# Attention pass of a graph kernel: bias moved into the indicator product, sigmoid read from PSUM, running sum placed before the next layer's dots

## The chip, the cores and the metric

The kernel runs on one core of a Trainium2 chip. The time is the device time of one execution in microseconds (us); what is compared is the median of several executions. The engines are PE (TensorE), DVE (VectorE), ACT (ScalarE), POOL (GpSimd) and SP (SyncE, which here only issues DMAs). Each engine works through its own instructions in order and waits for the others by semaphores.

## The reference, cut to what matters

The program is two graph networks, one after the other, over 100,000 nodes of 128 channels and 50,000 edges sorted by destination. The change touches only the first of them, three layers of graph attention:

```
def _gat_conv(x, src, dst, W, a_src, a_dst, b, n_nodes):
    h = x @ W
    s = h @ a_src
    d = h @ a_dst
    e = s[src] + d[dst]
    e = where(e > 0, e, 0.2 * e)
    w = exp(e - segment_max(e, dst)[dst])
    denom = segment_sum(w, dst)
    alpha = w / (denom[dst] + EPS)
    return segment_sum(alpha[:, None] * h[src], dst) + b
...
for m in range(3):
    x = x + sigmoid(_gat_conv(x, src, dst, Ws[m], att_src[m], att_dst[m], bias[m], n))
```

Every node has a loop to itself beside its edges, so a node without an edge has the closed form x + sigmoid(x @ W + b). The kernel computes that for all nodes in a first stage and then replaces the rows of the nodes that have edges.

## The kernel before

**Stages.** A dense stage over all nodes takes the first 1400 us. Then each of the three layers m has two passes over the edges: a first pass that gathers the source rows and takes their dots with the attention vectors, a short chain that turns scores into weights (`w`, denominators `slU`, their reciprocals), and a second pass that sums the rows and writes the new ones. After 6400 us comes the second network, which the change leaves alone. The change touches the second passes.

**Rounds.** The edges are cut into 392 columns of 128, and U = 8 columns make a round, so each pass has R = 49 rounds. `p_rounds` writes the first three rounds out, then a hardware loop whose body is four rounds, then the last ones. Inside `p2_round(i, rr, h)` every engine handles pieces of up to four different rounds, so the program is a software pipeline: for layer m, r = m * R + i.

**PE**, in the order of a round i: the product of the running sums of round i-1 with W into `pCW`'s PSUM bank (L1188, needs the scan of round i-1); the sums of round i, eight pairs of products `bXs x pA` and `pXd x bSW` (L1194, L1195, need masks and diagonals of round i); for round i-1 eight pairs `pAT x W` and `pIN x pCW` (L1204, L1206); the keys of round i+2 laid out along the columns (L1180). `pIN` holds in rows 0 to 7 an indicator of which column still belongs to the segment that a running sum carries on; all other rows are zero.

**ACT**: copies `pCW` (L955), copies the sums of round i out of PSUM to `pAT` (L964), writes eight diagonal matrices `bSW` for round i+1 (L949), and takes the sigmoid of round i-1 in place in SBUF, two groups of four columns (L970). In the last layer it first applies eight ReLUs with the normalisation of round i-2 (L959).

**DVE**: copies key fields for round i+2 (L1629); masks `pA` of round i+1 (L1637); for round i-2, in layers 0 and 1, sixteen dots with the next layer's attention vectors (L1653, L1655) and their copy to `SC` (L1659); copies `pFL` (L1663); the running sum of round i (`scan`, L1461, needs ACT's copy of the sums of round i); for round i-1 eight times PSUM * 1/denominator + bias into `bTH` (L1675, semaphore p_z); then, once the scatter of two rounds earlier has left the buffer, the addition of the node's own row (L1689). In the last layer come the second residual and the normalisation statistics (L1694 to L1706).

**POOL** issues eight indirect scatters for each round, one for each column (L770); in the last layer it first computes the reciprocal deviations (L783 to L787). **SP** issues in a round i: two loads of rows for round i+1 (L520, L523), the indicator of round i (L538), and in layers 0 and 1 the store of the new rows of round i-1 (L548). In the last layer it loads the residual rows too (L544).

## Time and profile before

| what | us |
|---|---|
| median of 3 runs | 13333.38 (13315.89 to 13337.69) |
| the profiled execution | 13224.56 |
| its span, first to last instruction | 13222.7 |
| second pass of layer 0, about | 2649 to 3410 |
| second pass of layer 1, about | 4060 to 4800 |
| second pass of layer 2, about | 5440 to 6410 |

The profiled execution is 0.8% below the median of the runs. Shares of the span: PE 51%, DVE 39%, ACT 30%, POOL 50%. They are averages over stages with different limits, so that the second passes are read by themselves: by windows inside them, by the waits in those windows, and by single rounds of the timeline. A wait "<-issue" or "<-remote" is idle time that the profile puts down to nothing, or to no engine of this core.

### The profile page before, as it was taken

Reading aid. Unit: us, or ns where it says so; the run is one execution under the profiler, and the core shown is the slowest. Engines: PE = TensorE matmul, PEld = TensorE weight load, DVE = VectorE, ACT = ScalarE, POOL = GpSimd, SP = SyncE. Lnnn points to the kernel's source line nnn. Section 1 sums busy time; section 2 is a strip of 40 time slices with the busy share of each in tenths; the row PEclk is TensorE's granted clock in tenths of the full one; section 3 lists DMA queues with packets and bytes.
Section 4 is the critical chain, followed back from the end, with each engine's and each line's share of the span. In section 5 each row is a group of like instructions: output and inputs, shape, how many; then the busy total and the mean of one; then the engine's idle time right before and its main releaser. Section 6 shows DMA issues by size and latency. Waiting matters only on the chain.

```text
span 13222.7 us, 165920 instructions
## 1 busy us (share of the span) xinstructions
PE 6805.4 (51%) x35028; PEld 5020.9 (38%) x35028; DVE 5117.0 (39%) x21443; ACT 3990.4 (30%) x8589; POOL 6568.4 (50%) x6253
## 2 busy tenths in 40 slices
PE   6777200077205730355322247777445888444888
PEld 3333100066205630355322235555333555333666
DVE  6777422366315641455322234443112333111444
ACT  7999300033102310233200024443112444111443
POOL 3444566544664566444677743233665333665000
PEclk9999655588657865677555568888556999555999
DMA  6777666644574457533233345565445777444998
GB/s 219 264 262 264 220 237 237 227 126 125 194 261 158 129 174 257 179 119 121 67 45 45 45 117 201 202 202 189 60 58 128 240 234 236 83 58 88 272 268 256
DMA packets 2128228, 2270.53 MB, mean 172 GB/s; under 512 B 234960, under 2 KB 1554869, under 8 KB 2121824
## 3 DMA queue, kind: packets, MB, share of 16 engines
q1 hardware_dynamic: 1798266, 1848.65, 42.2%
q0 software_dynamic: 321440, 418.37, 15.0%
q10 hardware_dynamic: 8390, 2.21, 0.1%
q14 instruction: 105, 0.86, 0.0%
q8 instruction: 27, 0.44, 0.0%
HBM read 1067.73 MB, written 1222.73 MB: 173 GB/s over the span
## 4 chain that ended last, share of the span: by engine, by line
DMA 14%; issue 11%; PE 8%; another core or an unknown queue 5%; POOL 4%; DVE 4%; SPq 3%; POOLq 1%; DVEq 0%; ACT 0%; ACTq 0%
DMA agg_d<-dO,fOI 10%; PE ps L1290 5%; DMA bXd<-agg_d 3%; POOL bO L810 2%; POOL agg_d L801 2%; PE ps L1267 2%; SPq L595 1%; DVE aO L1809 1%; PE ps L1277 1%; DVE bXd L1782 1%; PE ps L1265 1%; SPq L593 1%; DVE eE L1803 1%; SPq L602 0%
## 5 line engine op out<-in xcount | busy, mean ns | idle before, releaser
L862 POOL DMA_INDIRECT bXs<-x_d,fGI x784 | 798.6, 1019 | 1494.8 <-DMA x_d<-aH 1279.9
L801 POOL DMA_INDIRECT agg_d<-dO,fOI x784 | 1212.1, 1546 | 530.9 <-ACT dO L982 296.9
L1290 PE MATMUL ps<-W,aT 128*128 128x128 f32 x9408 | 1206.4, 291 | 22.8 <-ACT aS L999 15.6
L1277 PE MATMUL ps<-aS,W1X 128*128 128x512 f32 x2352 | 1207.4, 594 | 5.4 <-DMA eET<-eaT_d 5.2
L1290 PEld LDWEIGHTS ps<-W,aT 128*128 128x128 f32 x9408 | 1181.7, 208 | 39.7 <-ACT aS L999 25.9
L982 ACT COPY dO<-ps 128x128 f32<-128x128 f32 (+1 forms) x1176 | 318.2, 271 | 2733.7 <-DMA agg_d<-dO,fOI 1526.6
L1817 DVE TENSOR_TENSOR aH<-ps,B 128x512 f32<-128x512 f32 x588 | 406.4, 692 | 1848.1 <-PE ps L1290 1151.8
L1246 PE MATMUL ps<-bO,bNE 128*128 128x128 f32 x1568 | 568.9, 473 | 1021.5 <-ACT dO L982 1010.0
L1005 ACT ACTIVATE aT<-ps,BNT,BNS 128x512 f32<-128x512 f32 x1176 | 882.4, 774 | 609.2 <-PE ps L1278 574.7
L747 POOL DMA_INDIRECT bXs<-x_d,bGI x784 | 784.3, 1000 | 392.8 <-issue 247.7
L1246 PEld LDWEIGHTS ps<-bO,bNE 128*128 128x128 f32 x1568 | 382.5, 305 | 1198.1 <-issue 912.2
L1511 DVE CUSTOM_DVE_ANT_0 bTL<-bXs,VR 128x128 f32<-128x128 f32 x1176 | 290.1, 288 | 1411.6 <-DMA bXs<-x_d,bGI 803.2
L942 ACT ACTIVATE aYG<-aYG 98x512 f32<-98x512 f32 x3 | 1.9, 630 | 2444.1 <-DVEq L1605 2444.1
L1064 PE MATMUL ps<-aT,W 128*128 128x512 f32 x1176 | 616.1, 619 | 181.4 <-DVE aT L1411 181.3
L1733 DVE TENSOR_SCALAR bNE<-ps,dK 128x128 f32<-128x128 f32 x1176 | 317.7, 343 | 1007.8 <-PE ps L1224 1005.4
L801 POOL DMA_INDIRECT agg_d<-dO,dOI x392 | 618.7, 1578 | 153.4 <-issue 118.2
L770 POOL DMA_INDIRECT x_d<-bO,bOI x400 | 395.5, 989 | 519.3 <-DVE bO L1689 398.5
L1267 PE MATMUL ps<-ident,aO 128*128 128x128 f32 x2352 | 425.2, 321 | 365.8 <-DVE aO L1809 340.4
L1094 PE MATMUL ps<-ident,SC 128*98 128x128 f32 x12 | 3.3, 428 | 1173.4 <-DVEq L1570 1173.4
L1195 PE MATMUL ps<-bSW,bXd 128*128 128x128 f32 x2352 | 593.3, 343 | 26.4 <-issue 26.4
L1094 PE MATMUL ps<-ident,self_score 128*98 128x128 f32 x12 | 3.3, 430 | 1170.7 <-DVEq L1556 1170.7
L1012 ACT ACTIVATE aH<-aH 128x512 f32<-128x512 f32 x392 | 246.7, 630 | 1082.7 <-DVE aH L1817 713.5
(260 smaller groups left out, 17793.7 us busy)
## 6 DMA issues: line engine op xcount, KB each, us to landing
agg_d<-zeros SPq DMA_DIRECT2D x788, 256.0 KB
bXd<-agg_d SPq DMA_DIRECT2D x784, 256.0 KB
agg_d<-zeros SPq DMA_DIRECT2D x394, 290.0 KB
bXd<-agg_d SPq DMA_DIRECT2D x392, 290.0 KB
x_d<-aO SPq DMA_DIRECT2D x392, 256.0 KB, 2.1
yg_d<-aYG SPq DMA_DIRECT2D x196, 512.0 KB, 3.1
aX<-yg_d SPq DMA_DIRECT2D x392, 256.0 KB, 4.2
x_d<-aH SPq DMA_DIRECT2D x392, 256.0 KB
```

The lines of the kernel that those rows point to most:

```text
L747: pool.indirect_dma_start(bXs[:, s, u, :], None, gat_src[m], bass.IndirectOffsetOnAxis(ap=bGI[:, s, 1 if m == 0 else 0, u:u + 1], axis=0), ...
L770: pool.indirect_dma_start(gat_out[m], bass.IndirectOffsetOnAxis(ap=bOI[:, s, u:u + 1], axis=0), bOs[s][:, u, 0:wid], None, bounds_check=n_ ...
L801: pool.indirect_dma_start(agg_d[m][u % 2], bass.IndirectOffsetOnAxis(ap=index, axis=0), dO[:, u, 0:AW[m]], None, bounds_check=agg_last, oo ...
L862: pool.indirect_dma_start(fX[:, s, u, 0:C], None, gin_in[m], bass.IndirectOffsetOnAxis(ap=fGI[:, s, u:u + 1], axis=0), bounds_check=n_last ...
L1005: act.activation(eZ[:, k, h, :], ps[2 + 2 * k + h][:, :], ACT.Relu, bias=BNT[:, m, h:h + 1], scale=BNS[:, m, h:h + 1]).then_inc(e_zr, 1)
L1064: pe.matmul(ps[2 + k][:, :], W[:, m, :], aT[:, k, m, :], start=True, stop=True).then_inc(a_mm, 1)
L1195: mm = pe.matmul(cols(2 + u // 4, u % 4), pXd[:, rr, u, :], bSW[:, u, :], start=False, stop=True)
L1246: pe.matmul(ps[2 + u % 4][:, 0:C], dS[:, u, :], message_slot(s)[:, u, :], start=True, stop=True).then_inc(d_acc, 1)
L1267: mm = pe.transpose(ps[k][:, j * P:(j + 1) * P], eS[:, k, j, :], ident[:, :])
L1277: pe.matmul(z, W1X[:, m, h * P:(h + 1) * P], eHT[:, k, :], start=True, stop=False)
L1290: mm = pe.matmul(ps[6 + k][:, j * P:(j + 1) * P], eZ[:, k, h, j * P:(j + 1) * P], W2[:, m, h, :], start=(h == 0), stop=(h == 1))
L1817: v.tensor_tensor(eO[:, k, :, :], ps[6 + k][:, :].rearrange("p (j c) -> p j c", j=J), bias, ALU.add).then_inc(e_v, 1)
```

## The change

The bias is no longer added by DVE. The denominators, already in the slab `slU`, are stored to a DRAM buffer `den_d`; each round loads its eight columns of them as one row into partition 32 of `pIN`, and partition 32 of `pCW` holds the layer's bias. The product L1206, which always ran over 128 rows, then adds denominator * bias, and the later multiplication by the reciprocal leaves the bias. ACT takes the sigmoid straight from PSUM with the reciprocal as scale column, eight instructions of 128 columns, and does so before the diagonals of the next round. DVE loses L1675; its copy of `pFL` and its scan stand before the dots. SP issues one more DMA in each round, and at the start of each pass stores `den_d`, waits for it, and issues the first row loads only once the denominators stand.

```diff
+    den_d = dram("den_d", (R, U * P))
...
 SP, round i
                         sp.dma_start(pIN[0:U, s, :], ind_d[bass.ds(i, 1), :, :].rearrange("o u n -> (o u) n")
                                      ).then_inc(l_ix[s], 16)
+                        sp.dma_start(pIN[32:33, s, :], den_d[bass.ds(i, 1), :]).then_inc(l_ix[s], 16)
...
 SP, start of a pass
+                sp.wait_ge(z_v, ZV * (m + 1))
+                sp.dma_start(den_d.rearrange("r (h n) -> (r h) n", h=2), slU).then_inc(s_den, 16)
                 load_rows_of(0, 0)
+                sp.wait_ge(s_den, 16 * (m + 1))
...
 ACT, round i
+                    if inside(i - 1):
+                        act.wait_ge(p_fl, r)
+                        if past(i - 2):
+                            act.wait_ge(p_o, 2 * (r - 1))
+                        for u in range(U):
+                            if u % 4 == 0:
+                                act.wait_ge(p_rw, 2 * (r - 1) + u // 4 + 1)
+                            ins = act.activation(bTH[:, u, :], ps[4 + u // 4][:, (u % 4) * P:(u % 4 + 1) * P], ACT.Sigmoid,
+                                                 scale=pFL[:, 1 - s, 1, u:u + 1])
+                            if u % 4 == 3:
+                                ins.then_inc(p_sg, 1)
                     if inside(i + 1):
                         diagonals(i + 1, 1 - s)
-                    if inside(i - 1):
-                        for g in range(2):
-                            act.wait_ge(p_z, 2 * (r - 1) + g + 1)
-                            act.activation(bTH[:, 4 * g:4 * g + 4, :], bTH[:, 4 * g:4 * g + 4, :], ACT.Sigmoid).then_inc(p_sg, 1)
...
 ACT, start of a pass
+                act.copy(pCW[32:33, :], GB[32:33, m, :]).then_inc(p_cb, 1)
...
 PE, round i
                         if past(i - 2):
-                            pe.wait_ge(p_z, 2 * (r - 1))
+                            pe.wait_ge(p_sg, 2 * (r - 1))
...
 DVE, round i: the block "if inside(i)" (pFL, scan) now stands before the block of the dots; and
-                    if inside(i - 1):
-                        for u in range(U):
-                            if u % 4 == 0:
-                                v.wait_ge(p_rw, 2 * (r - 1) + u // 4 + 1)
-                            ins = v.scalar_tensor_tensor(out=bTH[:, u, :], in0=ps[4 + u // 4][:, (u % 4) * P:(u % 4 + 1) * P],
-                                                         scalar=pFL[:, 1 - s, 1, u:u + 1], in1=GB[:, m, :], op0=ALU.mult,
-                                                         op1=ALU.add)
-                            if u % 4 == 3:
-                                ins.then_inc(p_z, 1)
```

ACT, one round in the loop of layer 0, before. `pCW` and `bA` are the copies out of PSUM, `bSW` the diagonals of the next round, `bTH` the argument of the sigmoid.

```order
L955 COPY pCW<-ps 8x128 [waits p_cw]
L963 ISA
L964 COPY bA<-ps 128x512 [waits p_ag]
L963 REGISTER_ALU
L964 COPY bA<-ps 128x512 [waits p_ag]
L947 REGISTER_ALU
L949 ACTIVATE bSW<-ident,pFE 128x128 [waits p_fe]
L949 ACTIVATE bSW<-ident,pFE 128x128 x7
L970 ACTIVATE bTH<-bTH 128x512 [waits p_z] x2
```

The same round of ACT in the changed kernel.

```order
L961 COPY pCW<-ps 8x128 [waits p_cw]
L969 ISA
L970 COPY bA<-ps 128x512 [waits p_ag]
L969 REGISTER_ALU
L970 COPY bA<-ps 128x512 [waits p_ag]
L978 ACTIVATE bTH<-ps,pFL 128x128 [waits p_rw,p_o,p_fl]
L978 ACTIVATE bTH<-ps,pFL 128x128 x3
L978 ACTIVATE bTH<-ps,pFL 128x128 [waits p_rw]
L978 ACTIVATE bTH<-ps,pFL 128x128 x3
L953 REGISTER_ALU
L955 ACTIVATE bSW<-ident,pFE 128x128 [waits p_fe]
L955 ACTIVATE bSW<-ident,pFE 128x128 x7
```

The sigmoids moved ahead of the diagonals, became eight, and wait for PE's products (p_rw) in place of DVE's (p_z).

DVE, from the end of the dots to the end of a round in the loop of layer 0, before.

```order
L1659 ISA [waits p_dt]
L1659 COPY SC<-bDT 128x2x8
L1663 ISA [waits p_z]
L1663 COPY pFL<-keys 128x16
L1668 COPY pC<-pC 128x1 [waits p_c,p_fl,p_ev]
L1461 SCALAR_TENSOR_TENSOR pC<-pFL,pC,bA 128x8
L1674 REGISTER_ALU
L1675 SCALAR_TENSOR_TENSOR bTH<-ps,pFL,GB 128x128 [waits p_rw]
L1675 SCALAR_TENSOR_TENSOR bTH<-ps,pFL,GB 128x128 x3
L1674 REGISTER_ALU
L1675 SCALAR_TENSOR_TENSOR bTH<-ps,pFL,GB 128x128 [waits p_rw]
L1675 SCALAR_TENSOR_TENSOR bTH<-ps,pFL,GB 128x128 x3
```

The changed kernel, from the end of the masks to the first dots.

```order
L1654 TENSOR_SCALAR aH<-ps,pFE 128x128 x3
L1667 REGISTER_ALU
L1668 ISA [waits p_sg]
L1668 COPY pFL<-keys 128x16
L1673 COPY pC<-pC 128x1 [waits p_c,p_fl,p_ev]
L1478 SCALAR_TENSOR_TENSOR pC<-pFL,pC,bA 128x8
L1681 ISA bTL,bDT<-bO,VR 128x128 [waits p_dc,p_o]
```

The scan (L1461, now L1478) stands between masks and dots, and nothing follows the dots but their copy and the last addition.

## Rows read from the trace of the kernel before

**Rows 1.** Windows in the three passes: length, busy PE, PEld, DVE, ACT, POOL (xcount), clock, DMA share, GB/s

```profile
2700.00:3340.00 640.00, 460.83 (x2991) 408.96 (x2990) 414.92 (x2267) 199.33 (x529) 316.16 (x322) 0.81 0.43 128
4110.00:4750.00 640.00, 480.29 (x3120) 424.26 (x3119) 432.75 (x2352) 206.19 (x546) 331.39 (x337) 0.83 0.42 132
5500.00:6300.00 800.00, 466.07 (x2893) 425.43 (x2894) 405.92 (x1618) 300.97 (x826) 393.74 (x434) 0.73 0.35 121
```

**Rows 2.** Groups by line, 2700 to 3340: xcount | busy us, mean ns | idle before

```profile
L770 POOL DMA_INDIRECT x_d<-bO,bOI x162 | 159.8, 986 | 180.7 <-DVE bO L1689 131.5 <-issue 49.2
...
L949 ACT ACTIVATE bSW<-ident,pFE 128x128 f32<-128x128 f32 x328 | 100.2, 391 | 0.0
L1675 DVE SCALAR_TENSOR_TENSOR bTH<-ps,pFL,GB 128x128 f32<-128x128 f32 x320 | 86.6, 343 | 27.6 <-remote 24.7 <-PE ps L1206 3.0
...
L970 ACT ACTIVATE bTH<-bTH 128x512 f32<-128x512 f32 x80 | 50.4, 630 | 255.5 <-DVE bTH L1675 252.6 <-issue 3.0
...
L1659 DVE COPY SC<-bDT 128x16 f32 x40 | 7.0, 175 | 88.6 <-remote 83.6 <-issue 2.9 <-DVE bDT L1655 2.1
```

**Rows 3.** Groups by line, DVE, 4110 to 4750

```profile
L1663 DVE COPY pFL<-keys 128x16 f32 x42 | 8.2, 195 | 0.0
```

**Rows 4.** Waits, 2700 to 3340: who waited for whom, us in total, times, longest

```profile
POOL x_d L770 <- DVE bO L1689: 131.5, 20, 11.0
PE ps L1180 <- issue: 121.1, 135, 4.3
...
DVE SC L1659 <- remote: 83.6, 27, 4.3
DVE pFE L1629 <- issue: 68.9, 10, 7.5
...
PE ps L1188 <- DVE pC L1461: 32.9, 13, 6.0
```

**Rows 5.** Waits, 4110 to 4750

```profile
DVE SC L1659 <- remote: 92.4, 33, 3.6
...
PE ps L1188 <- DVE pC L1461: 21.8, 8, 6.4
```

**Rows 6.** Timeline of a round of layer 0: start, length, engine, line [idle before]

```profile
2935.53 2.45 ACT L949 ACTIVATE bSW<-ident,pFE 128x128 f32<-128x128 f32 x8
...
2948.11 0.23 DVE L1461 TENSOR_TENSOR_SCAN pC<-pFL,pC,aYG 128x8 f32<-128x8 f32 x1
...
2948.92 0.80 PE L1194 MATMUL ps<-bNE,bXs 128*128 128x128 f32 x2
...
2950.39 1.40 DVE L1689 TENSOR_TENSOR bO<-bTH,bXd 128x512 f32<-128x512 f32 x2
```

**Rows 7.** Timeline, the end of that round

```profile
2959.19 0.27 PE L1180 MATMUL ps<-ident,pFE 128*128 128x128 f32 x1 [0.46 <-issue]
...
2962.85 0.17 DVE L1659 COPY SC<-bDT 128x16 f32 x1 [2.89 <-remote]
```

**Rows 8.** Timeline of a round of layer 2

```profile
5850.62 3.18 ACT L959 ACTIVATE aT<-aT,bNR,bRS 128x128 f32<-128x128 f32 x8 [12.49 <-POOL bNR L787]
...
5851.31 1.09 POOL L770 DMA_INDIRECT yg_d<-bO,bOI  x1 [0.73 <-ACT aT L959]
...
5863.02 0.17 DVE L1686 COPY bOI<-IDX 128x8 int32 x1 [5.88 <-DMA yg_d<-bO,bOI]
...
5868.63 0.24 POOL L783 TENSOR_SCALAR bRS<-bMV 128x8 f32<-128x8 f32 x1 [7.27 <-DVE bNG L1706]
```

**Rows 9.** Timeline, from the denominators of layer 0 to its first rounds

```profile
2636.93 3.35 DVE L1620 RECIPROCAL aYG<-aYG 98x512 f32<-98x512 f32 x1
...
2648.81 0.63 PE L1194 MATMUL ps<-bNE,bXs 128*128 128x128 f32 x2
...
2653.93 1.04 PE L1180 MATMUL ps<-ident,pFE 128*128 128x128 f32 x8
```

**Rows 10.** The page, 40 slices of the span: GB/s that the DMA engines moved

```profile
GB/s 219 264 262 264 220 237 237 227 126 125 194 261 158 129 174 257 179 119 121 67 45 45 45 117 201 202 202 189 60 58 128 240 234 236 83 58 88 272 268 256
```

More of the change, by code:

```diff
@@ L1216, in _ @@
                 keys_along(1, 1)
+                pe.wait_ge(p_cb, m + 1)
                 p_rounds(pe, p2_round)
@@ L1647, in p2_round @@
                         masks(i + 1, 1 - s)
+                    if inside(i):
+                        if past(i - 2):
+                            v.wait_ge(p_sg, 2 * (r - 1))
+                        v.tensor_copy(pFL[:, s, :, :], keys[:, 4:6, bass.ds(i * U, U)]).then_inc(p_fl, 1)
+                        v.wait_ge(p_ev, 2 * (r + 1))
+                        v.wait_ge(p_fl, r + 1)
+                        if m or past(i - 1):
+                            v.wait_ge(p_c, r)
+                        v.tensor_copy(pC[:, s, 0:1], pC[:, 1 - s, U:U + 1])
+                        scan(pC[:, s, 1:U + 1], pFL[:, s, 0, :], pAT[s][:, P - 1:U * P:P], pC[:, 1 - s, U:U + 1], ALU.mult,
+                             ALU.add).then_inc(p_c, 1)
                     if inside(i - 2) and m < M - 1:
@@ L1659, in p2_round @@
                         v.tensor_copy(SC[:, 1:3, bass.ds((i - 2) * U, U)], bDT[:, 0:2, :]).then_inc(p_dc, 1)
-                    if inside(i):
-                        if past(i - 2):
-                            v.wait_ge(p_z, 2 * (r - 1))
-                        v.tensor_copy(pFL[:, s, :, :], keys[:, 4:6, bass.ds(i * U, U)]).then_inc(p_fl, 1)
-                        v.wait_ge(p_ev, 2 * (r + 1))
-                        v.wait_ge(p_fl, r + 1)
-                        if m or past(i - 1):
-                            v.wait_ge(p_c, r)
-                        v.tensor_copy(pC[:, s, 0:1], pC[:, 1 - s, U:U + 1])
-                        scan(pC[:, s, 1:U + 1], pFL[:, s, 0, :], pAT[s][:, P - 1:U * P:P], pC[:, 1 - s, U:U + 1], ALU.mult,
-                             ALU.add).then_inc(p_c, 1)
-                    if inside(i - 1):
-                        for u in range(U):
-                            if u % 4 == 0:
-                                v.wait_ge(p_rw, 2 * (r - 1) + u // 4 + 1)
-                            ins = v.scalar_tensor_tensor(out=bTH[:, u, :], in0=ps[4 + u // 4][:, (u % 4) * P:(u % 4 + 1) * P],
-                                                         scalar=pFL[:, 1 - s, 1, u:u + 1], in1=GB[:, m, :], op0=ALU.mult,
-                                                         op1=ALU.add)
-                            if u % 4 == 3:
-                                ins.then_inc(p_z, 1)
                     if inside(i - 1):
@@ L1711, in _ @@
                 p_rounds(v, p2_round)
+                v.wait_ge(s_den, 16 * (m + 1))
                 if m < M - 1:
```

9 lines of the change are left out of this document (6 added, 3 removed).

## The prediction

> **What bounds the kernel now.** The change touches only the second passes of the three layers, so I read windows inside them first, then the groups and waits of the same windows, then single rounds of the timeline.
>
> In layer 0 the window of 640 us holds 40 rounds, since the copy at L1659 runs once in a round: 16.0 us a round. Layer 1 does 42 rounds in 640 us: 15.2 us [rows 1 to 3]. In layer 2 POOL does 11 instructions in a round (three for the deviations, eight scatters), 434 in 800 us: 39.5 rounds of 20.3 us [rows 1]. No engine is full. Per round of layer 0, PE is busy 460.83 / 40 = 11.5 us, DVE 10.4, ACT 5.0 [rows 1]. POOL's scatter takes 0.99 us and 49.2 / 162 = 0.30 us of issue, so eight need 10.3 us [rows 2]. That is the floor of a round however fast the rest is; POOL now also waits for DVE's last addition, 131.5 us in 20 of the 40 rounds, those of one buffer [rows 4].
>
> The remainder of a round is of two kinds. One is waiting for DVE. PE waits for the scan 32.9 us in 40 rounds, 0.82 us a round, in layer 1 21.8 / 42 = 0.52 us [rows 4, 5]. ACT waits for the bias step 252.6 us [rows 2], but that is ACT's rest, not the path. The other kind I call the slow stretch: near the end of a round several engines crawl together. The keys, eight short products, need 1.04 us when nothing hinders them [rows 9], yet they sit idle 121.1 / 40 = 3.0 us a round with no releaser, each product standing 0.4 us and more after the one ahead [rows 4, 7]. In the same microseconds DVE stands 2.89 us ahead of the copy after the dots, 83.6 / 40 = 2.1 us a round, and 92.4 / 42 = 2.2 in layer 1 [rows 4, 5, 7]. PE's 11.5 busy + 3.0 crawling + 0.8 waiting is 15.3 of the 16.0 us, and DVE's 10.4 + 2.1 + 1.7 at the loop's turn + 0.7 ahead of the bias step is 14.9. So both chains are nearly closed, and PE's is the longer one. This is what I build on: a microsecond taken from DVE is worth only what PE waits for DVE.
>
> Layer 2 is another loop. POOL has the deviations; ACT's ReLUs follow at 5850.62, the scatters of the round before start at 5851.31, eight times 1.28 us; DVE, idle 5.88 us, is let into the buffer at 5863.02 when they have landed; its additions and statistics end at 5868.63 with the next deviations [rows 8]. None of these steps is L1675.
>
> **The change, part by part.**
>
> *Bias step gone from DVE, scan ahead of the dots.* It removes eight instructions, 86.6 / 40 = 2.2 us of DVE a round [rows 2], and lets the scan run as soon as ACT has copied the sums, ahead of sixteen dots. PE's wait for the scan should vanish: 49 x 0.82 + 49 x 0.52 = 66 us over layers 0 and 1. DVE's chain falls to 12.7 us, so what is late next is PE itself. The bound on the other side: the crawl stays where it is and PE, arriving earlier, only crawls longer; then a half or none of it is won. I take the whole, because the longest waits for the scan (6.0 us, 6.4 us) are too long to be hidden in a 3 us crawl. -66 us, ends -66 and 0.
>
> *Eight sigmoids for two on ACT.* No row shows a sigmoid of 128 columns from PSUM. The nearest below is the diagonal, 128 columns with a scale column, eight in 2.45 us [rows 6]; above, the ReLU with scale and bias columns, eight in 3.18 us [rows 8]. Now they are 2 x 0.63 = 1.3 us [rows 2]. I take 2.45, since the operands are those of the diagonal but for the source: ACT goes from 5.0 to 6.2 us of busy time, far from full.
>
> *Sigmoids ahead of the diagonals.* This is a new wait, and what is queued behind it on ACT is the eight diagonals that PE needs for the next sums. The sigmoids wait for PE's last products of the round. After those come four sigmoids and the first diagonal, 4 x 0.31 + 0.39 = 1.6 us (2.0 with the ReLU's price). PE in that time does the keys, 1.04 us, and the step from scan to first sum, 2948.34 to 2948.92, 0.6 us: also 1.6 us [rows 6, 9]. So the new wait is 0 to 0.4 us a round; with the hop of a semaphore I take 0.2: 98 x 0.2 = +20 us, ends 0 and +39. If PE's keys crawl, they cover it whole; if the products themselves come late, see the slow rival.
>
> *The bias row.* One more DMA of 4 KB a round on SP. It is issued behind the indicator of the same round and needed a round later, as that is; queued behind it on SP are the store and the loads of the next but one round. The product L1206 ran over 128 rows before, so PE pays nothing. 0; were SP on the path, an issue of about half a microsecond would be 98 x 0.5 = +49 us, which belongs to the slow rival.
>
> *Start of a pass.* The first row loads now wait for the denominators. From the end of the reciprocals, 2640.28, to the first sum, 2648.81, are 8.5 us [rows 9]. Two loads of 512 KB at the window's 128 GB/s would need 8.2 us, at the 264 GB/s of the dense slices 4.0 us [rows 10]. I take 1 us for three passes, upper end 3 x 2: +1, ends 0 and +6.
>
> *Layer 2.* ACT's diagonals move 2.4 us later, and so do PE's sums; DVE's idle 5.88 us ahead of the buffer and PE's rest until the next masks (PE is busy 466.07 / 39.5 = 11.8 of 20.3 us [rows 1]) hide it. 0.
>
> Sum: -66 + 20 + 1 = -45 us. Against the profiled execution that is 13224.56 - 45 = 13180 us. The median of the runs lies 109 us above that execution; I assume that this offset is not in the second passes and put the same -45 on the median: **13288 us**. The forecast's own range is 13267 (-66) to 13345 (half the gain, all costs: -33 + 39 + 6).
>
> **The rivals.**
>
> *The crawl sets the round (no change).* If all engines advance at a common pace, the number of instructions decides. The windows hold 9099 and 9474 of them [rows 1], 227 and 226 a round. The change takes away eight and adds six: 1% of 15.6 us, 0.14 us, times 98 is -14: 13320. For it: all engines crawl at once, and the crawl is in both layers alike. Against it: equal counts, yet 0.8 us between the layers' rounds. 20%.
>
> *The loop's turn.* DVE stands 68.9 us in layer 0, ten times for up to 7.5 us, once every four rounds, ahead of L1629 with nothing to wait for [rows 4]; in layer 1 it does not, and that layer's round is 0.8 us shorter. The loop bodies of DVE shrink in the changed program, from 263 instructions to 231 in layer 0 and from 273 to 241 in layer 1. If the stand goes with that, layer 0 falls to layer 1's pace: 49 x 0.8 = 37 us, of which 49 x 0.3 = 15 are already in the scan waits. -45 - 22: 13266. 12%. The Trainium skill, in "Runtime: NRT & Kernel Launch", section "Instruction fetch mechanics", states that instructions come in blocks of 256, that most engines hold two, and that a branch to a block no longer held waits for a fetch. By that rule 231 instructions always fit in two blocks, 263 not always, and the stand goes; the trace shows that it is there in one layer and not in the other, not why.
>
> *DVE was the bound (much faster).* If the crawl is made by DVE and PE running densely together, thinning DVE shortens it, and a round may fall to 13 us, half way to POOL's 10.3. 49 x (3.0 + 2.2) = -255: 13078. For it: the crawl comes where keys and dots meet. Against it: PE's part, 14.5 us, has no DVE in it. 12%.
>
> *ACT becomes the bound (slower).* So far ACT writes the diagonals right after its copies of the sums, while PE still has its last products to do. Changed, they sit behind those products; where the crawl falls on those, all eight sigmoids, 2.4 to 3.2 us, and the first diagonal stand between the end of the crawl and the next sum, where PE has 1.6 us of its own: 1.2 to 2.0 us lost. In two of three rounds that is 98 x 0.67 x 1.6 = +105, the scan's gain being lost too since PE then waits for diagonals instead; with a little given back, +90: 13423. It decides the sign once PE waits over 66 / 98 = 0.7 us a round for diagonals. 17%.
>
> **How the numbers follow.** The forecast has 39%, the rivals 20, 12, 12 and 17. The predicted time is the forecast's. The range must leave out no more than 2 in 10: 13130 cuts off the "much faster" case (10%), 13400 most of the slow one (9%). About 0.2%, 27 us, is what a measurement of this kernel can tell from no change. Faster by more than that: 0.29 of the forecast's 0.39 and both faster rivals, 0.53. Within it: 0.20 and 0.09 from the forecast and its edge, 0.29. Slower: 0.17 and a little, 0.18.
>
> **What would show it.** Right: PE no longer waits for the scan in layers 0 and 1, the round is 15 us in both, layer 2 stays at 20.3, the crawl is still there with 2 to 3 us a round on PE. Wrong: PE waiting for ACT's diagonals by more than 0.7 us (slow rival), a crawl much shorter (fast rival), a wait for `bXs` or `pXd` in the first round of a pass, or a layer 2 round that moved. If no loop of DVE stands at its turn any more, that rival was right too.

## The result, and the profile after

The changed kernel takes 13364.17 us (median of 9 executions, 13353.29 to 13371.48), the kernel before in the same comparison 13327.59 us (median of 9): a ratio of 1.0023 with a 95% interval of 1.0015 to 1.0032. It is slower by 37 us, where 45 us of gain were forecast. The two were later compared twice more, on chips called C and E below: 1.0007 (0.9998 to 1.0015) and 1.0012 (1.0003 to 1.0022). So the change costs nothing to 0.3%, and the question is where the gain went.

The profiled execution took 13364.17 us, with a span of 13362.6. The windows of the three second passes, to be held against [rows 1] (columns: length, busy PE, PEld, DVE, ACT, POOL, each with its count, then clock, DMA share, GB/s):

```profile
2720.00:3360.00 640.00, 446.21 (x2935) 407.10 (x2936) 332.30 (x1897) 231.48 (x760) 310.92 (x315) 0.79 0.42 124
4150.00:4790.00 640.00, 441.32 (x2988) 403.13 (x2986) 340.06 (x1958) 233.95 (x769) 319.15 (x323) 0.81 0.41 129
5580.00:6380.00 800.00, 473.56 (x2896) 431.65 (x2896) 322.71 (x1291) 341.31 (x1069) 394.44 (x433) 0.71 0.34 120
```

DVE got what it was promised: 332.30 / 40 rounds = 8.3 us instead of 10.4. ACT rose from 5.0 to 5.8 us. PE is less busy than before in 640 us, so it waits more. Layer 2 did not move: 433 instructions of POOL in 800 us, 20.3 us a round.

What PE and ACT waited for from 2700 to 3340 (who, for whom, us in total, times, longest), beside [rows 4]:

```profile
PE ps L1210 <- ACT bSW L955: 121.7, 24, 8.2
...
PE ps L1196 <- issue: 14.9, 20, 1.7
PE ps L1204 <- issue: 6.2, 9, 1.2
```

```profile
ACT bTH L978 <- remote: 157.7, 25, 10.0
```

The wait for the scan is gone: the product with the running sums, L1204, is never behind DVE. The slow stretch left the keys too, L1196, 14.9 us instead of 121.1. In their place stands one line: PE waits for ACT's diagonals (L955) ahead of the sums (L1210), 121.7 us, 3.0 us a round; layer 1 has the same line with 125.6 us in 30 waits. And ACT stands 157.7 us ahead of its sigmoids (L978), in 25 pieces of up to 10 us, with nothing that the profile can name.

Two groups by line, 2720 to 3360 (xcount, busy us, mean ns, idle before):

```profile
L978 ACT ACTIVATE bTH<-ps,pFL 128x128 f32<-128x128 f32 x320 | 89.4, 379 | 174.5 <-remote 157.7 <-PE ps L1222 8.6 <-issue 8.1
...
L1646 DVE COPY pFE<-keys 128x24 f32 x40 | 7.0, 174 | 35.0 <-ACT bSW L955 34.8 <-issue 0.2
```

The sigmoids themselves are cheap, 89.4 / 40 = 2.2 us a round for eight. The loop of DVE no longer stands at its turn: 0.2 us of issue ahead of L1646, where 68.9 stood ahead of L1629 [rows 4].

A round of layer 0 from the timeline (start, length, engine, line, in brackets the idle time ahead):

```profile
2958.58 0.39 PE L1222 MATMUL ps<-pCW,aO 128*128 128x128 f32 x2
...
2958.80 1.04 PE L1196 MATMUL ps<-ident,pFE 128*128 128x128 f32 x8
...
2961.33 0.29 DVE L1681 CUSTOM_DVE_ANT_0 bTL<-aT,VR 128x128 f32<-128x128 f32 x1 [0.61 <-issue]
...
2962.04 0.29 DVE L1683 CUSTOM_DVE_ANT_0 dO<-aT,VR 128x128 f32<-128x128 f32 x1 [0.41 <-issue]
...
2964.93 2.18 ACT L978 ACTIVATE bTH<-ps,pFL 128x128 f32<-128x128 f32 x8 [8.91 <-remote]
...
2966.94 2.47 ACT L955 ACTIVATE bSW<-ident,pFE 128x128 f32<-128x128 f32 x8
2967.51 0.50 PEld L1210 LDWEIGHTS ps<-bNE,bXs 128*128 128x128 f32 x2 [7.52 <-issue]
2967.54 0.77 PE L1210 MATMUL ps<-bNE,bXs 128*128 128x128 f32 x2 [7.35 <-ACT bSW L955]
```

By its record PE's last product of the round ends at 2958.97, and the keys, at full speed now, take 1.04 us. ACT might start its sigmoids then, but the slow stretch comes (DVE gets out one instruction in 0.71 us, the two dot products above), and ACT's first sigmoid starts at 2964.93. Then come eight sigmoids, 2.2 us, and only behind them the first diagonal, at 2966.94. PE has stood for 7.35 us.

What ACT stood for can be read, though no view prints it: the packed trace also keeps the time at which each semaphore was raised. The product that frees the first four sigmoids ends by its record at 2957.18, but its semaphore is raised at 2964.90, and the first sigmoid starts 0.03 us later; for the second four it is 2958.96 and 2965.80. Of the products of the round before, the last ends at 2948.77 and its semaphore is raised at 2948.78, so the two can also stand together. So ACT waits for PE's products, and their signal is up to 7.7 us late. Whether the products themselves were late or only their signal is not shown, since the ends of products are modelled.

About every second round goes like this one (24 waits for the diagonals in 40 rounds). In the others the stretch falls on PE's products and on ACT's copy of the sums. From one round's sums to the next it is about 15 and 17 us, mostly in turns. What comes in turns of 8.4 and 23 us in this trace are the running sums (L1478, at 2948.48, 2956.86 and 2980.35), which are not rounds; the expectation of `after_3` further down takes them for rounds.

### The profile page after: what moved, and what is told of

It reads as the page before. It is cut to its first block, busy times and chain, and to the rows that moved or that the text cites. A ratio compares the mean times of both kernels' runs of the same rounds, so it can differ in the third digit from the quotient of the medians.

```text
span 13362.6 us, 166188 instructions
## 1 busy us (share of the span) xinstructions
PE 6799.2 (51%) x35028; PEld 5047.7 (38%) x35028; DVE 4823.4 (36%) x20267; ACT 4127.8 (31%) x9474; POOL 6584.4 (49%) x6253
## 3 DMA queue, kind: packets, MB, share of 16 engines
q0 software_dynamic: 321440, 418.37, 14.9%
## 4 chain that ended last, share of the span: by engine, by line
DMA 14%; issue 11%; PE 8%; another core or an unknown queue 5%; DVE 4%; POOL 4%; SPq 3%; POOLq 1%; DVEq 0%; ACT 0%; ACTq 0%
DMA agg_d<-dO,fOI 10%; PE ps L1307 5%; DMA bXd<-agg_d 4%; POOL bO L816 2%; POOL agg_d L807 2%; PE ps L1284 2%; SPq L601 1%; DVE bXd L1791 1%; DVE aO L1818 1%; PE ps L1294 1%; SPq L599 1%; PE ps L1282 1%; DVE eE L1812 1%; SPq L608 0%
```

## How the experiments are read

The comparisons fell on different chips, here A to E; A is that of the first one, and whether it is one of the others is not known. The kernel before takes 13328 us on A, 13263 on B, 13266 and 13263 on C, 13261 on E and 12320 on D, so that only ratios to it on the same chip are compared. The table gives the length of a second pass in the profile of each kernel, from its first to its last product of the diagonals (L1195 of the kernel before), and in brackets that length / 48, the round. Each length is that of one execution; the same kernel differs in it by up to 12 us between chips for both layers together (1457 to 1469 us before).

| kernel | chip | layer 0, us | layer 1, us | ratio to before, 95% interval |
|---|---|---|---|---|
| before | A | 750.8 (15.64) | 718.5 (14.97) | |
| changed | A | 765.5 (15.95) | 755.4 (15.74) | 1.0023 (1.0015 to 1.0032) |
| base_again: before | B | 745.5 (15.53) | 711.8 (14.83) | 0.9994 (0.9985 to 1.0003) |
| early_sum_only | B | 752.4 (15.68) | 707.0 (14.73) | 0.9984 (0.9975 to 0.9993) |
| late_sum | B | 710.8 (14.81) | 707.7 (14.74) | 0.9951 (0.9938 to 0.9965) |
| dg_first | B | 688.9 (14.35) | 687.1 (14.31) | 0.9918 (0.9904 to 0.9932) |
| after_again: changed | C | 739.7 (15.41) | 743.7 (15.49) | 1.0007 (0.9998 to 1.0015) |
| late_dg | C | 712.0 (14.83) | 710.5 (14.80) | 0.9963 (0.9950 to 0.9976) |
| one_dot | C | 694.7 (14.47) | 680.5 (14.18) | 0.9935 (0.9919 to 0.9950) |
| half_rows | C | 691.9 (14.41) | 679.4 (14.15) | 0.9933 (0.9916 to 0.9951) |
| four_sc | C | 513.5 (10.70) | 504.0 (10.50) | 0.9653 (0.9635 to 0.9670) |
| one_scatter | C | 455.6 (9.49) | 438.9 (9.14) | 0.9536 (0.9521 to 0.9551) |
| before_one_sc | C | 563.9 (11.75) | 500.0 (10.42) | 0.9674 (0.9657 to 0.9691) |
| after_one_sc | C | 456.0 (9.50) | 445.1 (9.27) | 0.9549 (0.9532 to 0.9566) |
| quarter_rows | D | 475.7 (9.91) | 469.5 (9.78) | 0.9887 (0.9871 to 0.9902) |
| paused | D | 513.4 (10.70) | 505.5 (10.53) | 0.9966 (0.9953 to 0.9978) |
| base_3: before | E | 748.4 (15.59) | 718.2 (14.96) | 1.0002 (0.9993 to 1.0012) |
| after_3: changed | E | 738.6 (15.39) | 744.2 (15.50) | 1.0012 (1.0003 to 1.0022) |
| dg_first_3 | E | 685.4 (14.28) | 679.0 (14.15) | 0.9926 (0.9910 to 0.9943) |
| paused_3 | E | 688.2 (14.34) | 667.9 (13.91) | 0.9923 (0.9907 to 0.9940) |

Layer 2's pass lies between 944 and 948 us in every one of them. The profiled execution of `early_sum_only` was the slowest of its eleven (13270 us, median 13240), so its lengths do not show what its ratio shows. `after_again` was expected at 1.0015 to 1.0032 with rounds of 15.7 to 16.0 us; it came out at 1.0007 with 15.4 and 15.5.

## The order on ACT and on DVE

Theory A: the late diagonals are the new bottleneck. Theory B: all engines share a pace set by the number of instructions, and no order matters. The first four runs should separate them.

> The kernel before, unchanged, for a profile of one of its ordinary executions (the one shown of before, 13224.6 us, lay 0.8% under its other times). All theories: 13316 to 13340 us. New wait (A): the second passes of layers 0 and 1 take 751 and 719 us here as in the first profile, so that the change added 15 and 37 us to them. Own pace (B: the stretches in which all engines slow down set the mean round, whatever the order): they take some 10 to 25 us longer than in the first profile, because that one was a lucky execution, and the change then added less than 40 us in both together.

It is the kernel before, unedited. Its passes are 5 and 7 us shorter than in the first profile, not longer; about half of that is the chip (13263 against 13328 us). So the first profile was no lucky one in the second passes. What made that execution fast was not looked for.

`dg_first`, on ACT in `p2_round`:

```
+                    if inside(i + 1):
+                        diagonals(i + 1, 1 - s)
                     if inside(i - 1):
                         act.wait_ge(p_fl, r)
...
                                 ins.then_inc(p_sg, 1)
-                    if inside(i + 1):
-                        diagonals(i + 1, 1 - s)
```

> The changed kernel, with ScalarE's eight diagonals put ahead of the eight sigmoids again; nothing else. New wait (A: TensorE stands 3.0 us a round for diagonals because the sigmoids, which now wait for TensorE's own product, stand ahead of them): that wait goes, the round of layers 0 and 1 falls from 15.8 to at most 15.0 us, and the kernel takes 13280 us or less (36.5 to 80 us under 13364). Own pace (B): the wait for diagonals goes as well, but the slow stretch falls on another wait (keys again, or the masks), the round stays at 15.5 to 15.9 us and the kernel at 13350 to 13375 us.

13149.74 against 13262.87 us. Two lines moved, and the round falls from between 15.4 and 15.9 us to 14.3. Theory B expected no change and falls. The ratios, 0.9918 against 1.0007 to 1.0023 for the changed kernel, put the gain at 0.9 to 1.1%, more than A's own 0.3 to 0.6%.

`late_sum`: the block with the copy to `pFL` and the scan goes behind the dots again, where it was before.

> The changed kernel, with the running sum behind the dot products again; bias row and sigmoid from PSUM stay. Order as forecast (my prediction): TensorE waits again 0.8 us a round for the scan, +66 us less what the other waits hide: 13400 to 13430 us. Own pace (B): no difference, 13350 to 13375 us. New wait (A): between, since TensorE now stands for the diagonals behind the sigmoids and these wait for the product that the scan releases: 13364 to 13400 us.

13198.02 us, 0.9951. All three expectations missed: undoing the early sum makes the changed kernel faster. So the early sum is harmful beside late diagonals. What PE waited for from 2700 to 3340:

```profile
PE ps L1222 <- issue: 68.9, 101, 1.2
PE ps L1220 <- issue: 66.1, 97, 1.2
PE ps L1210 <- ACT bSW L955: 8.2, 13, 1.8
```

With the sum late, the slow stretch falls on PE's products themselves, 135 us in small pieces. By the time they are done it is over, and ACT's sigmoids and diagonals follow at once: 8.2 us of wait instead of 121.7. With the sum early, the records of PE's products have ended when the stretch comes, their signal is late, and the sigmoids ahead of the diagonals wait for it.

`early_sum_only`: the same block of the kernel before, moved ahead of its dots; bias step and sigmoids as before.

> The kernel before, with only the running sum moved ahead of the dot products. Order as forecast: TensorE's wait for the scan (0.8 and 0.5 us a round) goes, 13328 - 66 = 13262 us. New wait (A): the sigmoids stay behind the diagonals here, so nothing takes the gain away: 13262 to 13300 us. Own pace (B): 13315 to 13340 us, as before, with the slow stretch somewhere else.

13240.47 us, 0.9984: 22 us of gain, under A's 28 to 66, and more than B's none. Neither was right. PE, from 2700 to 3340:

```profile
PE ps L1194 <- issue: 68.8, 21, 4.8
PE ps L1194 <- DMA bXd<-xhc_d: 44.5, 13, 4.3
```

The scan is no longer waited for here either, but the stretch and the row loads now stand ahead of the sums, for 2.8 us a round.

`late_dg`: both moves undone, bias row and sigmoid from PSUM kept.

> The changed kernel with both orders as they were before: diagonals ahead of the sigmoids, running sum behind the dots; bias row and sigmoid from PSUM stay. It completes a square: after 15.9 us a round (sum early, diagonals late), diagonals first 14.35, sum late 14.8. Each order has its own price (A): the wait of TensorE for the scan comes back on top of the version with the diagonals first, 14.35 + 0.8 = 15.1 us a round, ratio 0.996 to 0.998. Only the pair early sum and late diagonals is bad (C: the sum ahead of the dots lets the product run early, sigmoids and diagonals then meet the slow stretch): this one is within 0.2 us a round of the version with the diagonals first, ratio 0.991 to 0.993.

0.9963, in the range of A in this text (each order has its own price, 0.996 to 0.998); its round of 14.8 us is under A's 15.1 and more than 0.2 us over 14.35, C's limit. PE's wait for the scan, 32.9 us in this window before, is 13.3 us here. So the four corners are, with the sum late, 14.8 us a round whichever way ACT is ordered, and with the sum early 14.3 us with diagonals first and 15.4 to 15.9 us with diagonals last. The two moves of the change are one gain and one loss that only exists with the gain.

## What the slow stretch is

`one_dot` is `dg_first` with only one of the 16 dot products of a round left, so that the next layer's weights come from stale numbers:

```
-                        for u in range(U):
-                            v.tensor_tensor_reduce(bTL[:, u, :], bOs[s][:, u, 0:C], next_d, ...
+                        for u in range(U - 1, U):
```

> Diagonals first, and of the 16 dot products of each round of layers 0 and 1 only one is left (15 VectorE instructions and 3 us of its time less a round; the softmax of the next layer gets stale numbers). Slow stretch made by how many instructions all engines issue (B): 288 instructions a round at 20.1 per us become 273, the round falls by 0.75 us, 72 us in 96 rounds, ratio 0.986. VectorE's own chain counts (C): its turn of masks, sum, dots and adds becomes 3 us shorter, up to 2 us a round fall out, ratio 0.977 or less. Neither: ratio as with the diagonals first, 0.992.

0.9935, like `dg_first` (0.9918, 0.9926). The window from 2700 to 3340:

```profile
2700.00:3340.00 640.00, 485.95 (x3243) 432.97 (x3241) 221.80 (x788) 251.79 (x827) 349.18 (x351) 0.84 0.46 139
```

DVE's busy time is 5.0 us a round (221.80 in 351 / 8 = 44 rounds), where the changed kernel has 8.3, and nothing came of it. So with eight scatters and the diagonals first, neither these instructions nor DVE's time sets the round.

A look into the kernel before, on chip E, where the stretch starts (of POOL the fifth, seventh and eighth scatter are shown):

```profile
2956.46 0.98 POOL L770 DMA_INDIRECT x_d<-bO,bOI  x1 [0.30 <-issue]
...
2957.82 0.29 DVE L1655 CUSTOM_DVE_ANT_0 dO<-bO,VR 128x128 f32<-128x128 f32 x1 [0.41 <-issue]
2957.84 0.27 PE L1180 MATMUL ps<-ident,pFE 128*128 128x128 f32 x1 [0.34 <-issue]
2958.53 0.08 DVE L1655 DVE_READ_ACCUMULATOR2_ANT bDT<- 128x1 f32 x1 [0.41 <-issue]
...
2959.03 0.98 POOL L770 DMA_INDIRECT x_d<-bO,bOI  x1 [0.30 <-issue]
2959.26 0.27 PE L1180 MATMUL ps<-ident,pFE 128*128 128x128 f32 x1 [1.15 <-issue]
...
2960.32 0.98 POOL L770 DMA_INDIRECT x_d<-bO,bOI  x1 [0.30 <-issue]
...
2961.41 0.27 PE L1180 MATMUL ps<-ident,pFE 128*128 128x128 f32 x1 [1.13 <-issue]
2962.12 0.37 PE L1180 MATMUL ps<-ident,pFE 128*128 128x128 f32 x1 [0.44 <-issue]
```

The starts are spaced by multiples of 0.71 us on PE and on DVE alike (2957.82 to 2958.53, 2961.41 to 2962.12), whatever the instruction costs. POOL's scatters keep their 1.29 us. ACT is different: from 2957.62 its eight diagonals run in 2.45 us, at full speed, and in 640 us of this trace no two of ACT's instructions follow each other by 0.71 us, against some 66 pairs on DVE. ACT only stands and waits. The slow pace begins at about the fifth of eight scatters and is over about 2 us behind the start of the last. The DMA engines are not full in it: in the changed kernel their share is 0.37 from 2960 to 2967. So the next kernels take scatters away; whoever reads the rows later gets stale ones.

```
                         elif u % 4 == 0:
                             pool.wait_ge(p_o, 2 * (m * R + i) + u // 4 + 1)
+                        if m < M - 1 and u < U - 1:
+                            continue
```

> Diagonals first, and of the 8 scatters of each round of layers 0 and 1 only one is left (7 GpSimd instructions less a round and 7/8 of the scattered rows; the next layer then works on rows that were never written). Slow stretch made by instruction count alone (B): 7 of 288 instructions less, round 14.35 to 14.0 us, ratio 0.989. Slow stretch made by the descriptors or by the DMA traffic of the scatters (D): it goes or shrinks to under half, the round falls to 9 to 12 us, where the dense rounds of 8.4 us are, ratio 0.96 or less.

0.9536: 5 us of every round are gone. Not all of them are the stretch: eight scatters at 1.29 us keep a round at 10.3 us or more, one does not. The same edit in the kernel before and in the changed one:

> The kernel before, with one of the 8 scatters of each round of layers 0 and 1 left (the next layer works on rows that were not written). In its trace all engines fall to one or two instructions a microsecond from about the fifth scatter of a round to two microseconds behind the eighth. Scatters make the slow stretch (D): it goes, and VectorE's own work sets the round, since its eight bias operations are still there (its busy time without the slow stretch is about 9.8 us a round): 10 to 11 us, ratio 0.963 to 0.970. If the slow stretch has another source here: 13 us or more.

> The changed kernel, with one of the 8 scatters of each round of layers 0 and 1 left, as in the kernel before beside it. Without the slow stretch the terms of the prediction stand alone. If its terms (scan wait gone, VectorE 2 us a round freer, a small wait for diagonals) were right and only the slow stretch overturned them: a round of 8.5 to 9.5 us, 1 to 2 us under that of the kernel before with one scatter, ratio 0.950 to 0.956. If the late diagonals cost by themselves: TensorE waits over 0.5 us a round for them here too, and the round is at least 0.5 us over the 9.3 us of the version with the diagonals first.

0.9674 and 0.9549, both in the ranges given, as is the changed kernel's round; the kernel before has 11.75 us in layer 0, where 10 to 11 were expected. Windows from 2700 to 3050, first of `before_one_sc`, then of `after_one_sc`:

```profile
2700.00:3050.00 350.00, 275.89 (x2173) 258.92 (x2172) 296.48 (x1641) 144.35 (x382) 28.75 (x30) 0.91 0.48 140
```

```profile
2700.00:3050.00 350.00, 317.00 (x2739) 301.07 (x2738) 300.68 (x1775) 218.60 (x703) 36.27 (x37) 1.00 0.60 175
```

POOL's count is the number of rounds. In 350 us the kernel before does 30, the changed one 37: 11.7 against 9.5 us. Without the stretch DVE is the limit before: 296.48 of 350 us busy, and 44.1 us of standing at the turn of its loop, in two rows, the second put down to ACT though the stand is as long:

```profile
DVE pFE L1631 <- issue: 25.4, 4, 6.9
DVE pFE L1631 <- ACT bSW L951: 18.7, 3, 6.9
```

The change takes the stand and the eight bias steps away; as a whole it is worth 1.3% here. PE is busy for 317.00 of the 350 us then, and its granted clock is 1.00, the level of 2.4 GHz, where the windows of the kernel before and of the changed one have 0.79 to 0.83 in layers 0 and 1, a mix of both levels. PE's work of a round takes 317.00 / 37 = 8.6 us here and 446.21 / 40 = 11.2 us in the changed kernel with all scatters: 2.6 us a round. In the timeline above, PE stands for 7.35 us and starts again with a granted clock of 0.50, 1.2 GHz, with two products every 0.43 us, and two every 0.22 us from 2972.77 on. The clock does not explain what the late diagonals cost: `dg_first_3` has

```profile
2700.00:3340.00 640.00, 493.79 (x3308) 442.57 (x3308) 374.59 (x2120) 256.50 (x843) 352.74 (x354) 0.85 0.47 140
```

and 45 rounds in it, 11.0 us of PE's work a round, as good as the same. With one scatter, `one_scatter` has 321.04 us in 37 rounds, 8.7: close to half of the 5 us that the scatters cost is PE's own work at the lower clock. In `after_one_sc` PE's wait for the late diagonals is there too, and it is small:

```profile
PE ps L1212 <- ACT bSW L957: 30.5, 34, 1.7
```

That is 0.8 us a round, four times my 0.2, yet the round is within 0.15 us of the 9.49 and 9.14 us of `one_scatter`, which has the diagonals first. The late diagonals become expensive only with the stretch.

The late signals go with the scatters too. From the end of the record of PE's product to its semaphore, the median over layer 0 (2700 to 3340, or to 3050 with fewer scatters and on D) is 4.7 us in the changed kernel on A and 3.0 on E, 5.5 and 5.8 in the kernel before on A and E, 5.7 in `dg_first_3` and 5.6 in `half_rows`; in `late_sum`, where the products themselves crawl, half of the signals are on time. It is 0.01 us in all three versions with one scatter. In layer 2, which has eight scatters a round, it is 0.01 us in every kernel. So eight scatters alone do not make the stretch. Nor does the rate of the others: layer 2 has 10.7 recorded instructions per us, the changed kernel's layer 0 has 13.8, and `after_one_sc` 22.8 without any stretch. What must come together with the scatters was not tested.

> Diagonals first, with 4 of the 8 scatters of each round of layers 0 and 1 left. With 8 the round takes 14.35 us, with 1 it takes 9.3. Each scatter has its price: 9.3 + 5.05 x 3/7 = 11.5 us, ratio 0.971. Only the scatters from the fifth on in a row slow the others down: 9.3 to 9.8 us, ratio 0.955 to 0.958.

Here four scatters are left, u = 1, 3, 5 and 7. 10.70 and 10.50 us lie between both expectations: from one to four scatters a round grows by 0.4 us for each, from four to eight by 0.9 us for each. So a scatter has no constant price, and it is not that only the fifth and later ones cost.

`half_rows` scatters 64 of the 128 numbers of each row in layers 0 and 1:

> Diagonals first, all 8 scatters, but each row in layers 0 and 1 is scattered with 64 of its 128 numbers (256 instead of 512 bytes; the other halves stay unwritten). Bytes make the slow stretch: half of the 5.05 us goes, 11.8 us a round, ratio 0.973. The number of scattered rows or of GpSimd's instructions makes it: 14.0 to 14.5 us as with whole rows, ratio 0.990 to 0.993.

0.9933 and 14.2 to 14.4 us, as with whole rows. Half the bytes of the scattered rows change nothing.

The last two questions were whether it is the rows or POOL's instruction, and whether eight scatters in a row are needed:

```
-bOI[:, s, u:u + 1] ... bOs[s][:, u, 0:wid]
+bOI[0:np_, s, u:u + 1] ... bOs[s][0:np_, u, 0:wid]        # np_ = 32 in layers 0 and 1
```

> Diagonals first, all 8 scatters of a round, but each scatters only the rows of 32 of the 128 partitions in layers 0 and 1 (the other rows stay unwritten). The number of scattered rows makes the slow stretch: three quarters of the 5.05 us go, the round falls to 10.0 to 11 us, ratio 0.958 to 0.967. GpSimd's instruction itself makes it, however few rows it names: 14.0 to 14.5 us and 0.990 to 0.994.

```
                             pool.wait_ge(p_o, 2 * (m * R + i) + u // 4 + 1)
+                        if u == 4 and rest is not None:
+                            pool.wait_ge(p_c, rest)
```

> Diagonals first, all scatters whole, but GpSimd waits between the fourth and the fifth scatter of a round of layers 0 and 1 for the running sum of the round after the next, so that no eight stand in a row. Only a row of more than four makes the slow stretch (in the trace of the kernel before it begins at about the fifth): it goes or halves, a round of 11 to 13 us, ratio 0.968 to 0.985. Each scatter slows the others for itself: the stretch is cut in two and the sum of both is the same, 14.1 to 14.8 us, ratio 0.990 to 0.996; with the pause ScalarE's and VectorE's waits for free rows can make it slower, up to 1.0.

Both fell on chip D, on which the kernel before takes 12320 us, 7% less than elsewhere, and their ratios can't be set beside those of the other chips. Both rounds lie under every range given. `quarter_rows` is therefore inconclusive: its round is 0.8 us shorter than that of `paused` on the same chip, but neither `dg_first` nor the kernel before has a profile there. What D did show is that the program alone does not make the stretch. `paused` there, 2700 to 3050 (the pass ends at 3044), and PE's first wait from 2700 to 3000:

```profile
2700.00:3050.00 350.00, 294.95 (x2369) 280.88 (x2368) 256.89 (x1534) 179.83 (x606) 259.39 (x257) 0.94 0.62 184
```

```profile
PE ps L1212 <- DMA bXd<-xhc_d: 43.1, 21, 3.6
```

A round takes 10.7 and 10.5 us, no row with "issue" is among PE's waits of that window, what it waits for is its row loads, and its signals come 0.01 us behind the records. POOL, with 257 scatters every 1.29 us, has hardly a gap left: this is the floor of 10.3 us. The same program on chip E takes 14.3 and 13.9 us, 3.6 and 3.4 us more, which is a better measure of the stretch than the 5 us above. So the last four runs put the kernel before and three others on one chip:

> The kernel before, so that its profile stands beside those of the next three on the same chip. The last call fell on a chip on which the kernel before takes 12320 us, not 13263, so a first question is what differs there. If this call falls on such a chip: its round of layers 0 and 1 is under 13 us and the slow stretch behind the scatters is shorter or gone. If it falls on a chip as in the first calls: 14.8 to 15.5 us a round, the stretch as before.

> The changed kernel. On a chip with the long slow stretch: ratio 1.000 to 1.003 and rounds in turns of 8.4 and 23 us. On a chip where the stretch is short: the terms of the prediction stand nearly alone as they did with one scatter (12657 against 12825 us there, -1.3%), and the ratio is 0.985 to 0.997. If the ratio is 1.0 on the fast chip too, then the stretch is not what took the gain.

> The changed kernel with ScalarE's diagonals ahead of the sigmoids. On a chip with the long stretch: 0.990 to 0.993, 0.8 to 1.0% under the changed kernel, now on one chip. On a chip with a short stretch: the diagonals' place matters little (with one scatter the rounds were 9.3 to 9.5 us either way), within 0.3% of the changed kernel.

> Diagonals first with GpSimd's pause between the fourth and the fifth scatter, beside the same without the pause. Only a row of more than four scatters makes the stretch: over 0.5% under the version without the pause on a chip with the long stretch. Each scatter slows the others for itself: within 0.3% of it, or slower by the pause.

It was a chip with the long stretch, so what the change does on a chip like D was not seen. `dg_first_3` is 13165.30 us against 13275.31 for the changed kernel on the same chip, 110 us or 0.8% less. `paused_3` is as fast as `dg_first_3` (13154.69), but that doesn't answer its question. Its scatters, with the first of a row, two in the middle and the last, and the first of the next:

```profile
2912.36 1.09 POOL L778 DMA_INDIRECT x_d<-bO,bOI  x1 [4.84 <-DVE pC L1480]
...
2916.34 0.98 POOL L778 DMA_INDIRECT x_d<-bO,bOI  x1 [0.30 <-issue]
2917.62 0.98 POOL L778 DMA_INDIRECT x_d<-aT,bOI  x1 [0.30 <-issue]
...
2921.49 0.98 POOL L778 DMA_INDIRECT x_d<-aT,bOI  x1 [0.31 <-issue]
2928.00 0.98 POOL L778 DMA_INDIRECT x_d<-aT,bOI  x1 [5.53 <-DVE pC L1480]
```

The pause is there, but the last four scatters of one round (from `bO`) and the first four of the next (from `aT`) now follow each other without a gap. Eight still stand in a row, as in 38 of the 46 rows of this window, so whether shorter rows would help was not tested. On D, up to 113 stand in a row without a stretch. PE and ACT of `dg_first_3`, 2700 to 3340:

```profile
PE ps L1196 <- issue: 96.8, 130, 1.9
```

```profile
ACT bTH L980 <- remote: 186.2, 45, 7.3
```

This is the point of the whole case in two rows. ACT's sigmoids stand as long as ever, 186 us in 45 pieces. But the diagonals are already written, and no row of PE waits for ACT. The stretch itself is still there: 96.8 us on PE's keys, 2.2 us a round.

## Why the prediction was wrong

Forecast were -45 us. With the length of layers 0 and 1 together, the steps can be priced one by one: 1457 to 1469 us before (A, B, E), 1422.5 `late_dg` (C), 1364 to 1376 `dg_first` (E, B), 1483 the changed kernel on C and E (1521 on A). Where two chips are mixed, a price is good to about 10 us.

**Scan ahead of the dots, -66 us: near in one place only, under a condition that I did not see.** From `late_dg` to `dg_first` it is 1422.5 to 1370, -52 us, and the wait for the scan is gone in every version with an early sum. But that the size is near is partly luck: `late_dg` waits only 13.3 us for the scan in layer 0's window (0.3 us a round). In the kernel before, where the diagonals are first as well, the same move was worth 22 us: the stretch moved on to PE's sums. This is the other side that the forecast named ("PE, arriving earlier, only crawls longer") and did not take. Beside late diagonals it is a loss, from `late_sum`'s 1418.5 to 1483.

**Sigmoids ahead of the diagonals, +20 us: this is the step that failed.** I set ACT's 1.6 us of work against PE's 1.6 us of its own, from rows without the slow stretch, and held 39 us for the most it could cost. From `dg_first` to the changed kernel it is 1370 to 1483, +113 us, 1.2 us a round, on the first chip 1.5; on chip E alone the times say +110. The 0.2 us would have been 0.8 even without the stretch, as `after_one_sc` showed. The main error is in two sentences of that part, "PE in that time does the keys" and "If PE's keys crawl, they cover it whole"; the other bound of the scan's part has it too, "the crawl stays where it is". I took the stretch as a property of the keys, where it belongs to a time, during the last scatters and 2 us behind, and falls on whatever is due then. The signals that the sigmoids wait for fell into it, and the eight diagonals and PE stood behind the sigmoids.

**The rival "ACT becomes the bound" was the right mechanism.** It gave +90 us and decided the sign from 0.7 us of wait a round; the trace has 3.0 us. Its place for the stretch, on PE's products with all sigmoids behind it, is what the late signals show. Its +90 stood for the whole change, with the scan's gain lost. The change as a whole came to +37 us on A, +10 and +14 on C and E, because the loop's turn was right as well.

**The loop's turn: right.** DVE's stand fell from 68.9 to 0.2 us in layer 0, and packets of instruction fetch (queue 14) in the whole execution from 105 to 56. `late_dg`, in which both orders are as before and the bias step is gone from DVE, has layer 0 shorter by 36 us than `base_3` (748.4 to 712.0, chips C and E) and layer 1 by 8. The rival had said 37 for layer 0. Since layer 1, which never stood, gained 8 us by the bias step, some 28 of the 36 are the turn. The Trainium skill, "Runtime: NRT & Kernel Launch", section "Instruction fetch mechanics", has most engines hold two blocks of 256 instructions; that DVE's loop of 231 instructions has no such stand and the one of 263 has it agrees with it.

**"The crawl sets the round" and "DVE was the bound".** The first falls with `one_dot`, 15 dots a round less and no gain, and with `dg_first`, where an order alone is worth 0.9%. The second is false with all scatters (`one_dot` again) and true without them, where the change, DVE's relief above all, was worth 168 us (12825.41 to 12657.52). My -255 rested on a stretch that grows shorter with DVE's work, and it doesn't.

**Sigmoids' price, bias row, start of a pass, layer 2: right.** Eight sigmoids take 2.2 us (forecast 2.45). No row of PE's waits names the load of the bias row. From the end of the reciprocals to the first sums of layer 0 it is 8.5 us in both kernels (2639.49 to 2648.02 in `after_3`), so that the +1 was 0. Layer 2 is 944.7 us before and 945.7 changed in the first comparison.

So the sum, from the runs with all scatters on chips with the long stretch: about -44 for the bias step with the loop's turn in it, -52 for the early sum, +113 for the late diagonals: +17. That it adds up to the lengths of E (1466.6 to 1482.8, +16) says little, since the prices are differences along the same chain; the times of E say +14. The forecast had -66, +20 and +1, and nothing for the loop's turn.

**A version that beats both.** `dg_first`: 0.9918 and 0.9926 of the kernel before, on two chips. It computes the same and keeps everything of the change but the order on ACT.

## What to carry to other kernels

Before a wait is put ahead of work that another engine needs, look at what happens to the queue in its worst microseconds, not in its clean ones; a slack worked out from undisturbed rows says nothing on them. A stretch in which several engines crawl at once may belong to a time and not to the instruction it was found on: find what runs just ahead of it (take that away once), and then order each engine's queue so that in this time nobody waits for anybody. When an engine waits for nothing that a view can name, compare the end of the producer's record with the time of its signal. And when an experiment is to break up a pattern, look in its trace whether it did: the pause only moved the row of eight. Two moves that are good alone or harmless alone should be measured as a square of four, since here the loss exists only in one corner.

## What the runs showed of the hardware

With eight indirect scatters a round on POOL in layers 0 and 1, PE and DVE fall together to one instruction in 0.71 us or a multiple of it, from about the fifth scatter to about 2 us behind the start of the last. ACT doesn't crawl but waits for signals: the semaphores of PE's last products are raised 3.0 to 5.8 us behind the end of their records (medians in layer 0, kernel before, changed and `dg_first_3`), and 0.01 us with one scatter. The round is 3.4 to 3.6 us longer on E than on D for the same program, and 5 us longer than with one scatter; PE's own work is 2.3 us longer a round in it, at a granted clock of 0.85 instead of 1.00. Half the bytes of each row change nothing. POOL itself keeps its 1.29 us. Layer 2 has eight scatters too, and neither the late signals nor another length in any kernel.

Chip D hardly shows it in the two versions profiled there, and the two kernels timed there and elsewhere (the kernel before and `paused`) are 7% faster on it, outside these passes too: layer 0's second pass starts at 2530 us instead of 2651. What the stretch is made of stays open: rows written or scatter instructions (the run for it fell on that chip), whether shorter rows of scatters avoid it, what layer 2 has different, and whether the recording of the trace has a part. The Trainium skill, "NOTIFIC — the notification-queue block", section "7.1 Overflow: three behaviours, one of which stalls the engine", says that the block that writes trace records holds its producers back rather than lose a record inside. That would slow recording engines in common, but no run here shows whether it does.
